# Value tree of a hard-routed feed-forward layer: from all sixteen leaves per token to tokens sorted by leaf

## What is computed

```
def _fff(x, node_w, node_b, w1, b1, w2, b2):     # 4096 tokens, 16 leaves, hidden width 64
    cur = zeros(N)
    for _ in range(4):                           # a walk down a tree of 15 nodes
        score = (xf * node_w[cur]).sum(-1) + node_b[cur]
        cur = 2 * cur + 1 + (score >= 0)
    sel = one_hot(cur - 15, 16)
    hidden_all = relu(einsum('nd,ldh->lnh', xf, w1) + b1[:, None, :])
    hidden = hidden_all * sel.T[:, :, None]
    return einsum('lnh,lho->no', hidden, w2) + sel @ b2

q, k, v = _fff(x, q...), _fff(x, k...), _fff(x, v...)
attn = softmax(q @ k.T / sqrt(128))              # within each batch of 1024 tokens
return attn @ v
```

## Time and profile before

| | us |
|---|---|
| median of 3 runs | 1772.68 |
| the profiled execution, whole | 1777.06 |
| its span in the trace | 1775.1 |
| phase trees, first instruction to the last copy | 554.2 to 844.8 |
| of it from the first `choose` on | 563.2 to 844.8 |

### The profile page before, as it was taken

The page is one execution under the profiler, slowest core; times in us unless marked ns, Lnnn a source line. Parts: engine busy times, 40 slices in busy tenths (PEclk is TensorE's granted clock), DMA queues, the critical chain, the costliest instruction groups (busy, mean ns, idle before and its releaser), DMA issues. The chain is left out here.

```text
span 1775.1 us, 47344 instructions
## 1 busy us (share of the span) xinstructions
PE 1583.7 (89%) x18858; PEld 1007.3 (57%) x18858; DVE 1472.8 (83%) x2120; ACT 1260.1 (71%) x2523; POOL 814.2 (46%) x1480
## 2 busy tenths in 40 slices
PE   5599999998966999999899549999999999999966
PEld 3366666666655877877687314444444444444544
DVE  7688889898665999988676768999999999999734
ACT  6378878787843445444665728998888888889955
POOL 6488878888935010000340424444444444444446
PEclk9699999999966999999999858999999999999978
DMA  7522232323273566664000441111121121112031
GB/s 250 203 79 89 89 94 88 97 88 98 59 141 56 93 96 91 92 90 63 1 1 0 152 178 48 60 52 59 55 69 54 56 70 53 58 53 71 25 77 48
DMA packets 119828, 141.86 MB, mean 80 GB/s; under 512 B 22205, under 2 KB 80698, under 8 KB 119610
## 3 DMA queue, kind: packets, MB, share of 16 engines
q1 hardware_dynamic: 119178, 138.78, 30.8%
q10 hardware_dynamic: 432, 0.07, 0.0%
HBM read 92.70 MB, written 44.98 MB: 78 GB/s over the span
## 5 line engine op out<-in xcount | busy, mean ns | idle before, releaser
L941 DVE TENSOR_REDUCE heads_mx<-heads_psM 128x1 f32<-128x1024 f32 x512 | 602.4, 1220 | 47.9 <-PE heads_psM L1032 31.9
L1012 ACT ACTIVATE heads_probs<-heads_psS 128x512 f32<-128x512 f32 x1024 | 546.1, 601 | 77.7 <-PE heads_psS L1055 71.7
L637 DVE TENSOR_REDUCE heads_mx<-heads_psM 128x1 f32<-128x1024 f32 (+7 forms) x512 | 356.4, 752 | 63.3 <-PE heads_psM L768 50.0
L981 POOL TENSOR_TENSOR heads_masked<-heads_probs,g_tri 128x128 f32<-128x128 f32 x512 | 233.8, 457 | 360.6 <-ACT heads_probs L1012 360.5
L721 ACT ACTIVATE heads_probs<-heads_psS 128x512 f32<-128x512 f32 x576 | 310.3, 604 | 83.6 <-PE heads_psS L733 78.8
L680 POOL TENSOR_TENSOR heads_probs<-heads_probs,one_ebias 128x512 f32<-128x512 f32 (+2 forms) x320 | 314.4, 999 | 61.5 <-ACT heads_probs L721 54.8
L1032 PE MATMUL heads_psM<-three_kS,three_qS 48*128 48x512 bf16 x1024 | 230.3, 394 | 20.4 <-PEq L2103 11.5
L1055 PE MATMUL heads_psS<-three_qS,three_kS 50*128 50x512 bf16 x1024 | 237.9, 389 | 0.7 <-ACT heads_probs L1012 0.3
L1563 ACT ACTIVATE trees_hid_hi<-trees_hid 128x512 fp32r<-128x512 f32 x192 | 121.7, 634 | 152.0 <-DVE trees_hid L1584 151.2
L794 PE MATMUL heads_psS<-one_qS,one_kS 50*128 50x512 bf16 (+3 forms) x768 | 151.5, 337 | 29.4 <-DMA one_qS<-heads_mrow 28.2
L1584 DVE SCALAR_TENSOR_TENSOR trees_hid<-trees_psH,g_b,trees_chosen 128x512 f32<-128x512 f32 x192 | 144.0, 750 | 31.2 <-DMA trees_chosen<-leaf_choice 13.5
(11 more groups left out here) (273 smaller groups left out, 3099.1 us busy)
## 6 DMA issues: line engine op xcount, KB each, us to landing
trees_chosen<-leaf_choice SPq DMA_DIRECT2D x96, 256.0 KB, 6.9
head_outputs<-g_small SPq DMA_DIRECT2D x128, 128.0 KB
one_qS<-q_parts SPq DMA_DIRECT2D x128, 96.0 KB
one_kS<-k_parts SPq DMA_DIRECT2D x128, 96.0 KB
three_qS<-q_parts SPq DMA_DIRECT2D x128, 96.0 KB
three_kS<-k_parts SPq DMA_DIRECT2D x128, 96.0 KB
q_parts<-g_w SPq DMA_DIRECT2D x8, 768.0 KB, 4.5
k_parts<-g_w SPq DMA_DIRECT2D x8, 768.0 KB, 6.0
```

The costliest lines, as they stand in the source:

```text
L637: last = dve.tensor_reduce(mx[:, p, qb:qb + 1], psM[(n * NM + i) % 2][:, at:at + w], AXX, ALU.max, negate=True)
L941: dve.tensor_reduce(mx[:, n % 2, k:k + 1], psM[k % 2][:, :], AXX, ALU.max, negate=True).then_inc(max_taken, 1)
L981: pool.tensor_tensor(masked[n % 2][:, kb, :], probs[n % 2][:, kb, kb * P:(kb + 1) * P], g["tri"][:, 0:P], ALU.mult).then_inc(near_done, 1)
L1012: act.activation(probs[n % 2][:, kb, h * CH:(h + 1) * CH], ring.bank(i)[:, :], ACT.Exp).then_inc(slot_taken, 1)
```

## The change

DENSE = 2: only trees q and k still go through the 128 dense tiles. The value tree is done so:

1. In route, ACT keeps `one_of`, the one-hot rows of tree v with tokens on partitions, and all 8 chunks of the normalised input `xn` stay in SBUF (in the place of `v_tok`). POOL clears a tile `zeros` and SP writes it three times, 1 MB each, over the HBM tensor `xs_dram` of SPAN = 4096 + 16*128 = 6144 rows.
2. In trees, during dense tiles 1 to 9, PE and DVE count the tokens of each leaf, round the counts up to 128, and find the row of each token in an order sorted by leaf (`pos`), and the leaf of each of the 48 tiles of 128 rows (`leaf_at`).
3. POOL writes the 4096 rows of `xn` to their places in `xs_dram` with 32 indexed transfers of 128 rows, and waits for all. Then it loads the sorted rows back, 12 groups of 512.
4. For each group k, in dense tiles 44+4k to 44+4k+7: PE turns the 4 tiles of rows, ACT copies, PE multiplies each with the weights of its one leaf (in f32, address from a register that PE loads from `leaf_at`, b1 by a 16-row matmul), ACT relu, PE turns, DVE copies, PE multiplies with w2 and b2 of the leaf, DVE copies, SP stores to `ys_dram`.
5. POOL reads the rows of each token back into `v_tok` with 32 indexed transfers, each for 128 tokens.

`bankA` and `bankB` take the place of `psV` and of the fifth `psH` (NP = 4).

```diff
-    NH, NT_, NM, NP = 4, 3, 3, 5
+    NH, NT_, NM, NP = 4, 3, 3, 4
-    CHUNKS = FF * NCH
+    CHUNKS = DENSE * NCH
+    COUNT_AT, BASE_AT, PLACE_AT, RANK_AT, ROW_AT = 1, 4, 6, 8, 44
+    def row_stage(n, late):
+        k = (n - ROW_AT - late) // 4
+        return k if (n - ROW_AT - late) % 4 == 0 and 0 <= k < GROUPS else None
...
 # POOL
+            pool.wait_ge(s["pos_ready"], 1)
+            for t in range(NT):
+                pool.indirect_dma_start(g["xs_dram"][:, :], bass.IndirectOffsetOnAxis(ap=pos[:, t:t + 1], axis=0),
+                                        xn[:, t // TPC, t % TPC, :], None).then_inc(s["scattered"], 16)
+            pool.wait_ge(s["scattered"], 16 * NT)
+            for k in range(GROUPS):
+                load(k)
+            for u in range(NX):
+                pool.wait_ge(y_stored[u], 16 * len(range(u, GROUPS, NX)))
+            for t in range(NT):
+                pool.indirect_dma_start(g["v_tok"][:, t, :], None, g["ys_dram"][:, :], bass.IndirectOffsetOnAxis(ap=pos[:, t:t + 1], axis=0)).then_inc(s["v_fetched"], 16)
+            pool.wait_ge(s["v_fetched"], 16 * NT)
...
 # PE
+            def which(j):
+                return pe.value_load(leaf_at[0:1, j:j + 1], min_val=0, max_val=(LEAVES - 1) * LW)
+            def turn_rows(k):
+                pe.wait_ge(x_loaded[k % NX], 16 * (k // NX + 1))
...
+                for t in range(TPC):
+                    last = pe.transpose(bankA[:, t * P:(t + 1) * P], xg[:, k % NX, t, :], g["identf"][:, :])
+            def first_layer(k):
+                pe.wait_ge(s["xT_ready"], k + 1)
+                for t in range(TPC):
+                    j = k * TPC + t
+                    out = bankA[:, t * LW:(t + 1) * LW]
+                    pe.matmul(out, of_leaf[:, j:j + 1].to_broadcast([LEAVES, P]), g["b1n"][:, :], start=True, stop=False)
+                    last = pe.matmul(out, xT[:, t * P:(t + 1) * P], g["w1"][:, V, bass.ds(which(j), LW)], start=False, stop=True)
+            def turn_hidden(k):
+                pe.wait_ge(s["leaf_ready2"], k + 1)
...
+            def second_layer(k):
+                pe.wait_ge(s["hidT_ready"], k + 1)
+                for t in range(TPC):
+                    j = k * TPC + t
+                    last = pe.matmul(bankB[:, t * P:(t + 1) * P], hidT[0:LW + 1, t * P:(t + 1) * P], g["w2s"][:, bass.ds(which(j) * 2, D)], start=True, stop=True)
             for n in range(TILES + LAG):
                 if n < TILES:
                     hidden(n)
                 if n >= LAG:
                     output(n - LAG)
...
+                for late, stage in ((0, turn_rows), (4, turn_hidden), (2, first_layer), (6, second_layer)):
+                    k = row_stage(n, late)
+                    if k is not None:
+                        stage(k)
...
 # SP, phase route
+            sp.wait_ge(zeros_ready, 1)
+            for i in range(ZERO_PARTS):
+                sp.dma_start(bass.AP(g["xs_dram"].tensor, i * ZEROS, [[ZERO_PARTS * ZEROS, P], [1, ZEROS]]), zeros[:, :]).then_inc(zeroed, 16)
             for c in range(NCH):
                 store_sel(c)
+            sp.wait_ge(zeroed, 16 * ZERO_PARTS)
```

More of the change, by code:

```diff
@@ L1284, in _ @@
             pool.memset(b2f[:, :, :], 0.0).then_inc(b2_cleared, 1)
+            pool.memset(zeros[:, :], 0.0).then_inc(zeros_ready, 1)
             for c in range(AHEAD):
@@ new lines, in _ @@
+            fill(ones, 1.0)
+            fill(after[:, 0:NT + 1], 0.0)
+            pool.iota(lane, pattern=[[0, 1]], base=0, channel_multiplier=LW).then_inc(s["made"], 1)
+            pool.iota(starts, pattern=[[P, ROWTILES]], base=0, channel_multiplier=0).then_inc(s["made"], 1)
+            keep(upper, P, 6)
+            keep(before, LEAVES, 7)
+            pool.wait_ge(g["w_loaded"][1], 32)
+            for k in range(2):
+                src = g["w1"][:, 1, :] if k == 0 else g["w2k"]
+                hi, lo = other[k]
+                pool.tensor_copy(hi[:, :], src).then_inc(w_hi, 1)
+                pool.wait_ge(w_hi, k + 1)
+                pool.tensor_tensor(lo[:, :], src, hi[:, :].bitcast(F32), ALU.subtract).then_inc(w_lo, 1)
@@ L1520, in output @@
                 pe.wait_ge(lo_ready, n + 1)
[L1521 to L1530 removed]
+                pe.matmul(ps[:, :], w2_hi[:, rows_], hid_lo[n % NH][:, :], start=False, stop=i == HID - 1).then_inc(used, 1)
@@ new lines, in count_leaves, with find_bases @@
+            def count_leaves():
+                pe.wait_ge(s["made"], MADE)
+                pe.wait_ge(s["made_v"], 1)
+                for t in range(NT):
+                    last = pe.matmul(bankA[0:LEAVES, 0:NT + 1], one_of[:, t, :], after[:, NT - t:2 * NT + 1 - t], start=t == 0, stop=t == NT - 1)
+                last.then_inc(s["counted"], 1)
+            def find_bases():
+                pe.wait_ge(s["padded_ready"], 1)
+                pe.matmul(bankA[0:LEAVES, P:P + 1], before, padded, start=True, stop=True).then_inc(s["based"], 1)
@@ new lines, in find_places @@
+            def find_places():
+                pe.wait_ge(s["reach_ready"], 2)
+                pe.matmul(bankB[:, :], upper, one_of[:, :, :].rearrange("p t l -> p (t l)"), start=True, stop=False)
+                for i in range(2):
+                    last = pe.matmul(bankB[:, :], ones, reach[:, i, :, :].rearrange("p t l -> p (t l)"), start=False, stop=i == 1)
+                last.then_inc(s["placed"], 1)
+                pe.wait_ge(s["leaf_ready"], 1)
+                pe.matmul(bankA[0:1, 2 * P:2 * P + ROWTILES], step, of_leaf[:, :], start=True, stop=True).then_inc(s["leaf_summed"], 1)
```

262 lines of the change are left out of this document (202 added, 60 removed).

## The result

| | before | changed |
|---|---|---|
| median us | 1773.22 (1771.41 to 1773.98) | 1829.34 (1827.85 to 1831.83) |
| ratio | | 1.0324, interval 1.0307 to 1.0342 |
| profiled execution: time, span, clock | 1777.06, 1775.1, 0.939 | 1828.21, 1826.5, 0.916 |
| first `choose` of trees, start of wide | 563.17, 845.58 | 552.59, 893.34 |

From the first `choose` to wide it now takes 340.7 us where it took 282.4; 20 less were forecast, 58 more came. It is not in the 340.7.) These are the windows of the changed kernel (stretch, length, busy us and count of PE, PEld, DVE, ACT, POOL; PEclk, DMA share, GB/s): the phase, the writes, the groups, the reads.

The account below looks back on a forecast made before the run. PE was taken to set the pace of the phase trees, DVE 0.09 us per tile behind. Terms -97 + 55 + 5 + 8 + 8 + 1 = -20 gave 1752.7 us against the median of 1772.68, range 1733 to 1825.

Parts of the forecast that it names:

- What goes, sorting, route: Value tree's dense chunks and a shorter tail removed, -97 us; sorting in tiles 1 to 9, +5; route's additions, +1.
- PE's new work: Turns and f32 matmuls of the 12 groups among dense tiles: 4.6 us per group, +55 us.
- Register loads: Eight leaf loads per group on PE at 0.65 us each, 4.5 us covered: +8 us (0 to 100).
- B: Rival: register loads stall PE in the groups at 1.6 us each, 100 us in all, 1845; chance 0.12.
- Clock: PE's clock in the group tiles: full clock, 1.0, expected, with a fall left to a rival of chance 0.06.
- C: Rival: PE's clock halves in the group tiles, 62 us for 52 tiles plus 45 for group work, 1860; chance 0.06.
- Indexed transfers: POOL's 32 writes and 32 reads at 1.5 us each: writes 3 late, reads 5.5 late, +8 us (0 to 99).
- A: Rival: each indexed transfer waits out a DVE instruction, 2.2 us instead of 1.5, +25, 1798 us; chance 0.24.
- a wait of 3: At tile 44, PE waits 3 us for the first sorted rows because the indexed writes end late.
- The tail: At the phase's end, the last indexed read lands 5 us behind the last copy.
- the bounds (0 to 99): Limits on the +8 us for indexed transfers, from issue prices of 0.59 to 2.92 us each.

Follow-up runs that it names:

- Sets 3 and 4: Two later sets of runs repeating the changed kernel unchanged, on chips 10 and 11: 1784.0 and 1784.2 us, without stalls.
- sets 5 and 6: Two later sets of runs repeating the changed kernel unchanged, on chips 9 and 13: 1825.9 and 1826.1 us, with both stalls.
- e4: Changed kernel without the value tree's groups, register loads and indexed transfers, sorting and two dense trees kept: 1676.4 us.
- e7: Changed kernel with each group's stages in four different tiles, the two layers apart, all 96 register loads kept: 1761.7 us, ratio 0.9943.
- e8: Changed kernel with the stages in four different tiles and each leaf's register loaded once and kept, 48 loads: 1759.5 us, ratio 0.9922.
- c2: Changed kernel run again unchanged as a control, no stall: 1784.2 us, ratio 1.0077.
- e3: Changed kernel with constants for the leaves in place of PE's register loads: 1766.7 us; run again, 1787.7.
- e1: Changed kernel with the 64 indexed transfers replaced by plain ones from the same queue, rows not sorted: 1769.8 us.
- set 4: The set of runs on chip 11: kernel before 1771.6 us, changed kernel unchanged 1784.2, without stalls.
- sets 1, 5 and 6: The first measurement and two later sets, in which the changed kernel unchanged took 1829.3, 1825.9 and 1826.1 us.
- sets 2, 3 and 4: Three sets of follow-up runs without stalls; the changed kernel unchanged, run in the last two, took 1784.0 and 1784.2 us.

## Why the prediction was wrong

1752.7 with 1733 to 1825 was forecast. The result, 1829.3, is above the range, and slower where faster was forecast. Sets 3 and 4 (1784) lie in the range, but also on the slower side, so the direction failed even without the stall; sets 5 and 6 (1826) are above it again. By its own steps:

- **What goes, sorting, route: right.** -95.7 by e4 against -97 + 5 + 1 = -91.
- **PE's new work: right at full clock.** 10.3 per group was forecast, e7 and e8 have 10.3 and 10.7 by turns, 12 x 0.2 = 2 us more. Its parts were off and cancel: the first layer takes 2.8 (0.36 for each pair of passes) instead of 1.9, the second 0.8 instead of 1.05, the eight turns 0.7 instead of 1.4. This much is luck.
- **Register loads: cost right, from two errors.** The sequencer's records of a load and its register operations add up to 0.52 us, but with the time between them the next load starts 0.77 behind (the two pairs of L1681 with gaps, above, are 0.77 apart). So eight take 6.2 and not 5.2, and they start 1.7 us ahead of the piece, so more is covered than 4.5. What shows in c2 is one or two gaps of 0.3 per group, near the forecast's 0.7. In e7 no matmul waits for one of 96. B (1.6 each) is out. The Trainium skill, "DMA: Bandwidth & Descriptors", section "Latency and other measured facts", gives a floor of some 600 ns; the trace does not bear it out as a floor, the load's own record is 0.30 us.
- **Clock: the step that failed on every occasion.** I gave C 0.06 because the earlier trace rows show f32 matmuls at full clock in long runs. The groups put 4.75 us of small ones between dense tiles. In c2 the periods average 12.46, in e7 10.9 (10.5 without two of them), by clock 0.88 against 0.98: 12 x 2.2 = 26 us over the 10.3 per group (the forecast had 8 of them, for register loads), of which putting the stages apart gives 19 back. It falls for some tiles behind a group, not for 52, so C's 62 + 45 was far too much. e3 run again shows the fall without any load, e7 full clock with all of them.
- **Indexed transfers: issue 1.26 us, not 1.5, landing far off.** A said that VectorE would keep POOL out. A transfer mostly takes 0.96 + 0.30 beside a VectorE busy 6 of 39 us and 35 of 37 alike (on average one per 1.29 and 1.30 us). The prediction read the Trainium skill, "SBUF — State Buffer", section "Who interferes with whom", too broadly: of `tensor_tensor`, an instruction with two SBUF inputs, it says that a probe did not see it stall transfers, since (inferred there) it takes only the shared read side and writing descriptors needs the other. `low` has two SBUF inputs too, and the trace agrees: it does not lengthen the issue. What is late is the landing, as c2 shows around tile 44:

```profile
620.15 0.96 POOL L1573 DMA_INDIRECT sorted_inputs<-g_v_tok,two_pos  x1 [0.30 <-issue]
...
629.43 1.61 POOL L1554 DMA_DIRECT2D g_w<-sorted_inputs  x2 [8.32 <-DMA sorted_inputs<-g_v_tok,two_pos]
...
639.58 1.12 PE L1652 MATMUL trees_bankA<-g_identf,g_w 128*128 128x128 f32 x4 [11.51 <-DMA g_w<-sorted_inputs]
```

  8.3 us from the end of the last issue to the last row, 10 more for the load, while the masks load through the same 16 engines; in the stalled trace, where no masks load, 1.6 and 3.7. The forecast had 5 for both and a wait of 3; PE waits 11.5, and that masks and rows share the engines was in the earlier trace rows (share 0.61). That the masks are the cause is argued from this comparison; no run moved them. e1, whose writes are issued sooner, does not wait, and its phase is 10 us shorter. The tail was right in sum, wide 4.9 behind the last copy's end where 5 was said; seen from that end, the reads are issued earlier than forecast and land later.

```profile
837.90 0.96 POOL L1581 DMA_INDIRECT g_v_tok<-sorted_outputs,two_pos  x1 [0.31 <-issue]
...
842.28 0.60 ACT L1705 ACTIVATE g_qkT<-trees_psO 128x512 f32<-128x512 f32 x1 [1.65 <-PE trees_psO L1618]
847.80 0.61 POOL L1955 CAST wide_v_hi<-g_v_tok 128x512 fp32r<-128x512 f32 x1 [8.94 <-SPq L1877]
```

- **The stall was in no rival.** It is worth 42 to 45 us. A asked whether VectorE holds up POOL; it went the other way round, over PE's increments. Nothing in the trace of before shows an indexed transfer, and the bounds (0 to 99) were put around POOL's time only, not around what the train does to others.

Sum for c2's phase: -95.7 + 12 x (12.46 - 5.68) + 11.5 for tile 44 + 5 of tail = +2 (5.68 being four dense tiles at 1.42); measured 285.6 - 282.4 = +3.2. The medians are 11 to 13 apart. For set 4 this is accounted for: the profiled executions are only 5.5 apart (1782.5 and 1777.1), that of before being 5.5 above the median of its kernel in this set and c2's 1.7 below its own.

## What to carry to other kernels

Put small matmuls between large ones in pieces as short as possible: the same work in two tiles instead of one kept TensorE at 2.4 GHz nearly throughout and turned +0.7% into -0.6%. Halving the register loads in the whole piece gave -0.6% too, and both together -0.8%, which is no clear difference. Let a train of transfers wait for the progress of what it serves, even where it need not: here it cost nothing that could be measured (2 us at most), and took 28 of 42 us when the train held up others. And measure a kernel on more than one occasion before believing a number for it; four executions within 0.3% of each other were here 45 us from the next eight.

## What the hardware showed that was not expected

- 32 indexed transfers back to back (one per 1.26 us) can delay PE's semaphore increments by up to 34 us (the matmul of `hidden(19)` ends at 581.3, its increment comes at 615.86), from the sixth to tenth transfer on, until some 5 us behind the last; VectorE's do not come late. That the increment and not the matmul is late is concluded from starts and updates. It came in sets 1, 5 and 6, there in the trace of every kernel with such trains, and in none of sets 2, 3 and 4.
- The clock of a repeating pattern has two rhythms: the program without register loads ran eight periods of 10.45 us on end and then, unchanged, one of 11.8 and one of 13.9; run again, seven of 13.4 to 13.9 with 1.2 and 2.4 GHz by turns.
- Loads of a register on PE, each with its register operations, follow each other 0.77 us apart, and four in a row are hidden where dense matmuls stand around them (e7).
